# Mamba units of 32 channels times four states, folded in four PSUM strips, with the products shared out anew over three engines, and a key mask in bf16

## The reference, cut to what matters

```
def ssm_scan(dt, Bm, Cm, x, A):              # E = 512 channels, NS = 16 states
    def step(h, inp):
        dt_t, B_t, C_t, x_t = inp
        dA = jnp.exp(dt_t[..., None] * A)                       # decay
        h = dA * h + (dt_t * x_t)[..., None] * B_t[:, None, :]  # B product, scan
        y = jnp.einsum('ben,bn->be', h, C_t)                    # C product, fold
        return (h, y)
...
qk = qk + padding_mask * -1000000000000.0
attn = jax.nn.softmax(qk, axis=-1)
```

## Time and profile before

| what | value |
|---|---|
| median of 3 runs | 3295.24 us (3292.39 to 3296.28) |
| the profiled execution | 3291.57 us, of which the span of the trace is 3289.6 us |
| PE busy | 2629.0 us (80%) |
| DVE busy | 2054.3 us (62%) |
| ACT busy | 1399.7 us (43%) |
| POOL busy | 1365.6 us (42%) |
| granted TensorE clock, mean | 0.902 of full speed |
| first scan to last scan of layer 0's mixers | 105.0 to 1088.6 us |
| the same in layer 1 | 2386.4 to 2865.0 us |

### The profile page before, as it was taken

The page is one execution under the profiler, slowest core; times in us unless marked ns, Lnnn a source line. Parts: engine busy times, 40 slices in busy tenths (PEclk is TensorE's granted clock), DMA queues, the critical chain, the costliest instruction groups (busy, mean ns, idle before and its releaser), DMA issues. The chain is left out here.

```text
span 3289.6 us, 27384 instructions
## 1 busy us (share of the span) xinstructions
PE 2629.0 (80%) x8344; PEld 1210.1 (37%) x8344; DVE 2054.3 (62%) x2826; ACT 1399.7 (43%) x2120; POOL 1365.6 (42%) x1134
## 2 busy tenths in 40 slices
PE   5788888888977687678887299996588897779976
PEld 2223323323322254323332278883233232235522
DVE  1799999999999443666662200013199999832233
ACT  4566566566554332225554022221455654322143
POOL 2587887887786301300001400004178878610000
PEclk8999999999999898879998599996799999976788
DMA  1220320220220000333312234542202202000000
GB/s 63 104 103 14 112 104 15 96 109 7 96 103 0 19 1 15 87 48 40 40 21 74 100 143 173 186 167 74 114 25 103 103 1 103 0 19 0 0 8 26
DMA packets 69056, 215.24 MB, mean 65 GB/s; under 512 B 13596, under 2 KB 38440, under 8 KB 49848
## 3 DMA queue, kind: packets, MB, share of 16 engines
q1 hardware_dynamic: 62536, 181.11, 17.0%
q10 hardware_dynamic: 3312, 24.12, 2.1%
q0 software_dynamic: 3072, 8.39, 0.8%
HBM read 187.97 MB, written 25.43 MB: 65 GB/s over the span
## 5 line engine op out<-in xcount | busy, mean ns | idle before, releaser
L750 POOL TENSOR_TENSOR s_dbu<-s_dx,s_bc 128x512 f32<-128x512 f32 x768 | 975.3, 1276 | 312.9 <-DVE s_psum L490 311.9
L420 PE MATMUL s_psum<-s_hc,ident 128*128 128x512 f32 x1536 | 849.4, 638 | 211.3 <-DVE s_hc L506 210.6
L639 ACT ACTIVATE s_psum<-s_dt,s_a_neg 128x512 f32<-128x512 f32 x768 | 526.5, 690 | 630.6 <-DVE s_hc L506 629.9
L506 DVE TENSOR_TENSOR s_hc<-s_psum,s_bc 128x512 f32<-128x512 f32 x768 | 523.3, 682 | 0.6 <-PE s_psum L420 0.3
L420 PEld LDWEIGHTS s_psum<-s_hc,ident 128*128 128x128 f32 x1536 | 239.8, 190 | 765.1 <-DVE s_hc L506 688.5
L490 DVE TENSOR_TENSOR_SCAN s_psum<-s_psum,s_state,s_dbu 128x512 f32<-128x512 f32 x384 | 494.4, 1287 | 10.2 <-ACT s_psum L639 10.2
L490 DVE TENSOR_TENSOR_SCAN s_psum<-s_psum,s_dbu 128x512 f32<-128x512 f32 x384 | 468.3, 1220 | 12.8 <-ACT s_psum L639 10.0
L1405 ACT ACTIVATE s_probs<-s_banks 128x512 f32<-128x512 f32 (+3 forms) x384 | 169.8, 493 | 206.9 <-PE s_banks L1228 163.8
L1775 ACT ACTIVATE s_hidden<-s_banks,s_w 128x256 f32<-128x256 f32 x184 | 77.2, 471 | 302.2 <-PE s_banks L1598 302.2
L381 PE MATMUL s_psum<-s_pad,s_taps 128*128 128x512 f32 x384 | 191.2, 592 | 0.0
L1329 DVE TENSOR_REDUCE s_umax<-s_banks 128x1 f32<-128x512 f32 (+3 forms) x256 | 138.9, 586 | 77.5 <-PE s_banks L1203 67.9
(11 more groups left out here) (250 smaller groups left out, 3505.0 us busy)
## 6 DMA issues: line engine op xcount, KB each, us to landing
s_bc<-fwd_rows SPq DMA_DIRECT2D x64, 1024.0 KB, 4.7
s_bc<-m_rows SPq DMA_DIRECT2D x32, 1024.0 KB, 4.7
s_w<-in_moe_w SPq DMA_DIRECT2D x23, 1028.0 KB, 7.2
s_w<-in_moe_w ACTq DMA_DIRECT2D x23, 1024.0 KB, 5.5
qk_parts<-s_parts SPq DMA_DIRECT2D x48, 128.0 KB, 1.8
s_stack_q<-qk_parts SPq DMA_DIRECT2D x48, 128.0 KB, 5.0
s_stack_k<-qk_parts SPq DMA_DIRECT2D x48, 128.0 KB, 8.3
moe_in_rows<-s_zero SPq DMA_DIRECT2D x1, 5888.0 KB, 18.8
```

The lines of the kernel that those rows point to most:

```text
L420: pe.matmul(psum[:, SCANS + block_no % 2, :], consts["ident"][:], hc[:, unit % PRODUCTS, :], start=(n == 0), stop=(n == NS - 1)).then_inc( ...
L506: dve.tensor_tensor(hc[:, unit % PRODUCTS, :], psum[:, unit % SCANS, :], bc[:, 2 * n + 1, :], ALU.mult)\
L639: act.activation(psum[:, unit % SCANS, :], dt[:, g % 2, i // NS, :], ACT.Exp, scale=a_neg[CHUNKS[g][0]][:, i:i + 1]).then_inc(decay_ready, 1)
L750: pool.tensor_tensor(dbu[:, unit % TERMS, :], dx[:, g % 2, i // NS, :], bc[:, 2 * n, :], ALU.mult)\
```

## The change

A unit is now 32 channels times four states: partition r * 32 + c holds channel c of the strip and state 4n + r. The numbers are split by `split(i)`: q the block of 128 channels, n the group of four states, j the strip of 32 channels. There are still 64 units in a chunk.

- The sum over states is now partly over partitions: `total` multiplies by `fold` (four identities of 32 on top of each other), 32 weight columns, into the strip j of the block's bank. The totals of four units stand together, after every fourth unit.
- dt and dx must stand four times on the partitions. They are stored to DRAM (`store_dt`, `store_dx`) and read back, each strip four times (`spread_dt`, `spread_dx`). The B and C rows come as tiles of 128 x 512 with four different rows (`spread_b`, `spread_c`).
- For the 32 units of a chunk with `TURNED` (i % 16 in 4 to 7 and 12 to 15) PE makes the B product: dx is transposed (`turn_dx`) and put back (`store_turned`), ACT makes diagonal matrices of B (`make_diag`), and `turn_term` runs 16 matmuls of 32 weight columns and 128 columns each into the four strips of the unit's PSUM bank. The decay then goes to `dbu` in SBUF. POOL makes the other 32 products.
- For the 34 units of a chunk with `LENT` the scan writes to `hc` in SBUF and POOL does the product with C (`weigh_lent`, four units behind) and, in the first chunk of a sequence, copies the kept state. DVE does the other 30.
- TERMS goes from 3 to 4 and PRODUCTS from 4 to 8; dt has one buffer for two. The lists of unit numbers of the other pieces are new: the convolution now comes two matmuls a unit for i below 8, `out` from i = 8 to 15, `rows` at 17 and 18, `in_z` from 28 to 35.
- In the masked cross-attention the product of -4e12 and the key mask is split in three bf16 parts and moved to three rows by DMA, and the mask matmul is bf16 with three rows.

```diff
+def split(i):
+    return i // NS, i // STRIPS % GROUPS, i % STRIPS
...
+            def turn_dx(g, b):
+                w = tile["turn", g, b]
+                pe.wait_ge(dx_ready, EB * (g + 1))
+                pe.wait_ge(work_free[w % 2], w // 2)
+                for q in range(EB):
+                    mm = pe.transpose(bank(w)[:, q * P:(q + 1) * P], dx[:, g % 2, q, b * P:(b + 1) * P], consts["ident"][:])
...
+            def turn_term(g, i):
...
+                for b in range(CH // P):
+                    for r in range(STRIPS):
+                        mm = pe.matmul(psum[r * STRIP:(r + 1) * STRIP, unit % SCANS, b * P:(b + 1) * P],
+                                       turned_dx(g)[:, q, b, j * STRIP:(j + 1) * STRIP], diag[:, at, r, b, :],
+                                       start=True, stop=True)
...
+                if LENT[i]:
+                    pe.wait_ge(product_lent, lent(unit + 1))
+                else:
+                    pe.wait_ge(product_ready, own(unit + 1))
+                pe.matmul(psum[j * STRIP:(j + 1) * STRIP, SCANS + block_no % 2, :], fold[:], hc[:, unit % PRODUCTS, :],
+                          start=(n == 0), stop=(n == GROUPS - 1)).then_inc(product_used, 1)
...
-                    total(g, i)
-                    if g + 1 < NC and i < 16:
-                        conv(g + 1, i // TAPS, i % TAPS)
...
+                    if i + 2 < UNITS and TURNED[i + 2]:
+                        turn_term(g, i + 2)
+                    if i % STRIPS == STRIPS - 1:
+                        for j in range(STRIPS):
+                            total(g, i - STRIPS + 1 + j)
+                    if g + 1 < NC and i < 8:
+                        conv(g + 1, i // 2, i % 2 * 2)
+                        conv(g + 1, i // 2, i % 2 * 2 + 1)
...
+                    if g + 1 < NC and i in (46, 47, 50, 51):
+                        turn_dx(g + 1, (46, 47, 50, 51).index(i))
+                    if g + 2 < NC and 52 <= i < 60:
+                        in_x(g + 2, (i - 52) // KD, i % KD)
...
-                    if g and i == 26:
+                    if g and i == 16:
                         add_res(g - 1, 0)
...
+            def store_turned(g, b):
+                w = tile["turn", g, b]
+                act.wait_ge(work_ready[w % 2], w // 2 + 1)
+                for e in range(EB):
+                    act.wait_ge(dx_stored[e], 16 * (g + 1))
...
-                    if g + 1 < NC and i in (36, 37, 40, 41):
-                        store_steps(g + 1, (36, 37, 40, 41).index(i))
+                    if g + 1 < NC and i in (26, 27, 30, 31):
+                        store_steps(g + 1, (26, 27, 30, 31).index(i))
...
-                    if g and post is not None and i == 44:
+                    if g and post is not None and i == 34:
                         log_var(g - 1)
...
+            store_cols(0)
+            for k in range(NS):
+                make_diag(0, 0, k)
+            for b in range(CH // P):
+                store_turned(0, b)
...
+            def weigh_lent(unit):
+                pool.wait_ge(scanned, unit + 1)
...
+                pool.tensor_tensor(at, at, c_rows[:, n, :], ALU.mult).then_inc(product_lent, 1)
...
-                            mm = pe.matmul(scores[:, u, hb, :], neg4[:],
-                                           key_mask[:, b, :].unsqueeze(1).to_broadcast([1, HB, SK]),
+                            mm = pe.matmul(scores[:, u, hb, :], ones3[:],
+                                           maskb[:, b, :].unsqueeze(1).to_broadcast([3, HB, SK]),
                                            start=False, stop=True)
```

More of the change, by code:

```diff
@@ L216, in _, with among, lent, own @@
                 act.activation(rstd[:, c, :], rstd[:, c, :], ACT.Exp, scale=-0.5).then_inc(rstd_ready, 1)
+STRIP = 32
+STRIPS = P // STRIP
+GROUPS = NS // STRIPS
 UNITS = EB * NS
-SCANS, TERMS, PRODUCTS = 4, 3, 4
+SCANS, TERMS, PRODUCTS, LAG = 4, 4, 8, 4
+DIAG = (1, 3)
+LENT = [i in LENT_AT for LENT_AT in ((1, 3, 4, 5, 7, 8, 9, 11, 12, 13), (1, 3, 4, 5, 7, 8, 9, 11, 12, 13), (3, 5, 7, 9, 12, 13),
+                                     (1, 3, 5, 7, 8, 9, 12, 13)) for i in range(NS)]
+TURNED = [i % NS in (4, 5, 6, 7, 12, 13, 14, 15) for i in range(UNITS)]
+MADE = [n for n in range(GROUPS) if not all(TURNED[n * STRIPS:(n + 1) * STRIPS])]
+KEEPS = sum(not (LENT[i] and LENT[i - 1]) for i in range(1, UNITS, 2))
+def among(table, units):
+    return units // UNITS * sum(table) + sum(table[:units % UNITS])
+def lent(units):
+    return among(LENT, units)
+def own(units):
+    return units - among(LENT, units)
+def turned(units):
+    return among(TURNED, units)
+def made(units):
+    return units - among(TURNED, units)
+def split(i):
+    return i // NS, i // STRIPS % GROUPS, i % STRIPS
 def mixers(core, consts, xn, res, x, runs, post):
@@ L451, in _ @@
                 steps_of(0, m)
+            turn_cols(0)
+            for b in range(CH // P):
+                turn_dx(0, b)
             for m in range(EB):
@@ new lines, in scan @@
+                if TURNED[i]:
+                    dve.wait_ge(term_turned, turned(unit + 1))
+                    left, right = right, left
+                else:
+                    dve.wait_ge(dbu_ready, made(unit + 1))
+                if LENT[i] and unit >= PRODUCTS:
+                    dve.wait_ge(product_used, unit - PRODUCTS + 1)
+                h = hc[:, unit % PRODUCTS, :] if LENT[i] else psum[:, unit % SCANS, :]
+                dve.tensor_tensor_scan(h, left, right, begin, ALU.mult, ALU.add).then_inc(scanned, 1)
@@ L539, in _ @@
                         keep(g, i)
-                    if unit:
+                    if unit and not LENT[(unit - 1) % UNITS]:
                         weigh(unit - 1)
@@ L642, in _ @@
-            act.wait_ge(small_loaded, 32 * len(runs))
+                    act.wait_ge(dt_spread[q % 2], 16 * STRIPS * (unit // NS // 2 + 1))
+                if TURNED[i]:
+                    to = dbu[:, unit % TERMS, :]
+                    if unit >= TERMS:
+                        act.wait_ge(scanned, unit - TERMS + 1)
+                elif unit >= SCANS and LENT[(unit - SCANS) % UNITS]:
+                    act.wait_ge(scanned, unit - SCANS + 1)
+                elif unit >= SCANS:
+                    act.wait_ge(product_ready, own(unit - SCANS + 1))
@@ L643, in _ @@
+            act.wait_ge(small_loaded, 16 + 32 * len(runs))
             for r in range(len(runs)):
@@ L688, in _ @@
+                    if g + 2 < NC and i in (58, 60, 62, 63):
+                        store_x(g + 2, (58, 60, 62, 63).index(i))
             if post is not None:
@@ L839, in cross_attention, with _ @@
         N_LOAD = (5 + 2 * B) * 16
+        @block.sync
+        def _(sp):
+            if not causal:
+                sp.wait_ge(mask_step, 5)
+                for part in range(3):
+                    sp.dma_start(maskb[part:part + 1, :, :], mask_parts[:, part, :]).then_inc(mask_stored, 16)
         @block.tensor
@@ L871, in _ @@
             pe.wait_ge(vd_ready, B)
+            if not causal:
+                pe.wait_ge(mask_stored, 3 * 16)
             with pe.Fori(0, B) as b:
```

354 lines of the change are left out of this document (255 added, 99 removed).

## The result

The changed kernel took 3472.79 us (median of 4 runs, 3461.01 to 3480.3), the kernel before 3294.78 beside it (3292.39 to 3296.28): a ratio of 1.054, 95% interval 1.051 to 1.057. I had forecast 3281 and a range up to 3360, so both the sign and the range were wrong.

The account below looks back on a forecast made before the run. DVE was taken to bound the mixers, PE close behind, and PE the masked cross-attention. 3291.6 - 60 (mask) + 17 (loops) + 30 (way in) = 3278.6, or 3282 on the median's scale, stated as 3281; range 3180 to 3360.

Parts of the forecast that it names:

- The mask: Masked cross-attention loop, 174.6 us before: three-row bf16 mask matmuls and a recovering clock gain 60 us.
- The way into the loop: Before each layer's first scan: dt and dx through DRAM and back cost some 15 us a call, +30 in all.
- The term: On PE: one turned term of 16 small matmuls takes 1.2 us, between estimates of 1.0 and 1.4.
- The walk: A middle chunk of layer 0, engines' in-order lists followed with every wait: 130.7 us against 122.5 before; 129 taken.
- The third quarter: Of a middle chunk: 33 us by the walk, 33.2 before, with ACT's chain to in_z's first bank some 8 us.
- Which chunks: Loops +17 us: six middle chunks of layer 0 +36, two of layer 1 +9, last chunks -14 each, first chunks 0.
- Rival 2: PE's first-quarter list decides in full, 8 to 12 us a middle chunk: 3320 in the middle, 3366 far end; chance 0.33.
- Rival 1: DVE and POOL set the pace in the loops, -70 to -115 us: 3167, up to 3200; chance 0.25.
- rivals 3 and 4: Strips do not overlap for the terms, 4100, chance 0.03; mask's clock stays, only 30 us go, 3311, chance 0.05.
- 85 at most: ACT's work in a middle chunk: 72.4 us busy before, plus 32 diagonals and four copies, 85 us at most.
- the bound of 31.8 for the first quarter: Lower bound for a middle chunk's first quarter, one of four bounds summing to 113 us against 122.5.

Follow-up runs that it names:

- Experiments 2: Changed kernel with each dt or dx repeat DMA split into four, 32 channels outermost instead of four: 3405.43 us, ratio 1.034.
- kernel 3: On top of Experiments 2, SyncE stores all four blocks of dt and dx before reading any back: 3361.73 us, ratio 1.021.
- re-tiling alone (5): kernel 3 without turned terms, diagonals or C products on POOL, seven product buffers, last B and C rows read earlier: 3314.98 us, ratio 1.007.
- no terms there (6): kernel 3 without turned terms in units 0 to 15, four C products on POOL there, last B and C rows earlier: 3303.7 us, ratio 1.004.
- half terms (4): Changed kernel with 8 of a turned term's 16 matmuls, part of the computation left out: 3420.39 us, one run.
- single totals (12): On top of re-tiling alone (5), each of the 64 totals issued alone instead of in groups of four: 3410.5 us, ratio 1.033.
- experiment 9: kernel 3 with ACT's four gate copies at units 32, 34, 36, 38 instead of 36, 38, 40, 42: 3348.22 us, ratio 1.014.

## Why the prediction was wrong, step by step

**The mask: right.** Taken at 60, it gave 53.0; clock 0.86, inside my 0.85 or more, and the loop 121.8, inside 110 to 125. The causal loop's 109.7 was not reached.

**The way into the loop: the mis-sized term.** I took 15 us a layer (up to 22) and it cost 54.6 and 53.7, 78 us more than the sum had in it. Two terms of the step failed: "an issue on SP takes 0.47", and "two waits of 2" for the stores. I priced the DMAs by their issues and never by the time their bytes take: 256 KB each, 2.6 us at the 100 GB/s of the trace, which is what an issue then took (10.02 for four); with wide DMAs an issue is 0.45 again. The 2 us for a store came from one of 64 KB with nothing ahead of it; these are 256 KB, stand behind the repeated rows and landed after some 10. Experiments 2 and 3 put the cause down: the layout of the DMAs 52 us of both prologues, the stores' place 29. With both mended 13 and 14 us remain. That scan 0 is then at 118.2, where I had said 120, is luck: with the stores in the order that I had counted it comes at 134.5, and in kernel 3 the path is another one. There ACT writes the first decay at 111.8, not at 118, and the scan waits for POOL's product, which stands until 116.8 for dx's repeated rows.

**The term: right.** 1.2 us taken, 1.01 plus 0.2 behind it measured between plain matmuls, and 0.90 where totals follow (843.29 to 844.19). The Trainium skill's page "TensorE: Matmul & The Clock Gate", section "Part 3: Packing small matmuls", says that a weight load overlaps a running matmul only if the row group is another one. This case's trace does not agree: the 32 weight loads of the term, all on the same rows, are busy 0.81 us of the 1.01 that the whole term takes. The 3.5 us that I had set beside that rule did not come.

**The walk: right in its mechanism, and talked down.** It said 34.7, 33, 33, 30; measured were 35.5, 32.8, 36.1, 29.6. Then I took 129 for 130.7, because "the walk adds every wait in full". It was 134.0. I had walked one chunk only: every second middle chunk of layer 0 has 36.7 in its second quarter, for 31.2 before. How well PE's list alone gives the first quarter (convolution 16 and `out` 8 matmuls by 0.86, a group of totals 1.0, a term 1.2, half a term 0.7):

| kernel | PE's list in units 0 to 15 | first quarter |
|---|---|---|
| re-tiling alone (5) | 20.6 + 4.0 = 24.6 | 29.9 |
| no terms there (6) | 24.6 | 29.2 |
| half terms (4) | 24.6 + 8 x 0.7 = 30.2 | 32.5 |
| changed kernel | 24.6 + 8 x 1.2 = 34.2 | 35.5 |
| single totals (12) | 40 x 0.86 = 34.4 | 35.3 |

With a list of 24.6 us the quarter does not follow it: in 5 DVE is busy 29.3 of 29.9, in 6 busy 26.8 with a wait of 2.4 for a decay. From 30.2 on it follows, 1 to 2 us above the list. Two unlike ways to load the same list give the same quarter, so it is the length of the list that counts, by whichever engine it reaches DVE: PE's terms in the changed kernel, ACT's decays in 12.

**The third quarter: 33 against 36.1.** The step that failed is what the wait for `in_z`'s bank costs. The wait, ACT's chain up to `log_var`, was in the walk; what follows it was not. Windows of PE in steps of 3 us, from 902.1:

```profile
902.10:905.10 3.00, 0.04 (x1) 1.00 0.26 102
905.10:908.10 3.00, 3.00 (x11) 0.65 0.26 101
...
920.10:923.10 3.00, 0.18 (x2) 1.00 0.01 3
923.10:926.10 3.00, 2.17 (x3) 0.50 0.00 0
926.10:929.10 3.00, 3.00 (x43) 0.50 0.04 14
```

And PE's own timeline there:

```profile
905.06 1.12 PE L517 MATMUL s_psum<-s_xn,s_w_in 128*128 128x512 f32 x2 [3.82 <-ACT s_dx L821]
906.11 1.93 PE L587 MATMUL s_psum<-s_hc,s_fold 128*32 128x512 f32 x8
907.97 1.83 PE L517 MATMUL s_psum<-s_xn,s_w_in 128*128 128x512 f32 x2
```

PE stood 3.8 us, and the group of totals behind it took 1.86 us (906.11 to 907.97) for 0.97 at full clock; after the next stand, 3.7 us for a group of products, the clock was 0.50, its lower level of 1.2 GHz, for six us. In the kernel before the clock in this quarter was 1.00 throughout. How much of the 3.1 us is this, I can't say: experiment 9 took 1.5 us from this quarter, where the wait for `log_var` stayed, and 4.8 from that of the first chunk, where its own wait went; and 12 shows a low clock that costs nothing where PE has room. This split stays open.

**Which chunks: wrong.** The loops took +119 for +17. Of the 102 missed, 29 went with the DMAs of experiments 2 and 3, whose late rows and late turned dx reach into the loops: most of what the two first chunks lost (+7.1 and +11.3, with the DMAs mended 1.9 and 3.0). The other 73, all by kernel 3: the six middle chunks of layer 0 +65 for my 36, the two of layer 1 +21 for my 9, the last chunks +1.0 and -2.4 for my -14 each, the first ones 5. Layer 1's first quarter is 35.5 us as well, as it has the same convolution, `out` and terms; I had credited it for waits that fall in other quarters. And I let the last chunks run at an engine's pace that their lists did not let them reach, though their last quarter did fall, from 28.1 to 23.5 by the starts of the scans.

**The rivals.** Rival 2 (PE's list in full, 3320 to 3366) was the mechanism, at its far end: +90 in the loops once the DMAs are mended (3361.73, which is kernel 3 and not the one forecast). 58 of the 90 go when terms and lent products do; the other 32 are there without any term, and which of the new places in the lists they come from is not shown beyond the wait at `add_res`. Its "DMAs I did not price" turned out to be the other half. Rival 1 (the pace of DVE and POOL) is refuted by DVE's 103.0 of 134.0 us; rivals 3 and 4 by the term and the clock. By the largest parts the miss is 3472.8 - 3281 = 192: way in 78, loops 102, mask 7, and some 6 us of the stages that I had left at nothing. Two sums of the forecast have flaws that moved nothing: ACT's 84.6 us already fill its "85 at most" without the four copies (82.0 measured), and the bound of 31.8 for the first quarter has no working.

## What to carry to other kernels

Price a DMA on the path by its bytes at the rate that a transfer of the same layout shows, and look first whether its outermost dimension is long: with 4 it moved 100 GB/s here, with 32 and no repeat inside over twice that. Where engines run in-order lists, add up one engine's list between two points that depend on each other, and trust that sum over a busy share of the whole; 120 us of DVE work taken to 103 was worth nothing while PE's list of one quarter grew from 27.5 us (32 matmuls by 0.86) to 34.2. When several good and bad parts come in one change, run them alone: the mask by itself makes this kernel 1.7% faster, inside the change it is lost.

## What the runs showed of the hardware

- DMAs that put rows on several partitions: 100 GB/s at a busy share of 0.2 to 0.3 with an outermost dimension of 4, 200 to 270 GB/s at 0.9 with one of 32 and no repeat inside, both in 2 KB packets, and 420 GB/s for the B and C rows before (128 copies outermost, 8 KB packets). At 100 GB/s four issues on SyncE took up to 10.0 us, with the wide ones 1.8.
- Sixteen fp32 matmuls of 32 output columns and 128 moving ones, four side by side, took 1.01 us in front of a plain fp32 matmul and 0.90 in front of another such group; two plain ones between two groups took 1.92 for 1.72.
- After PE had stood for 3.7 to 3.8 us its clock was 0.65 and 0.50 in the next 3 us, in the two cases shown; after the first, a group of totals took 1.86 us for 0.97.
- Matmuls of the mask with three bf16 rows in place of one fp32 row: the loop's clock went from 0.66 to 0.86, and to 0.92 in the kernel with the mask alone.
